# Attention: each part of the row maxima is sent as soon as it exists, not both parts after the second

## The reference

```python
x = x + xattn(layernorm(x), ctx, ctx, Wq, Wk, Wv, bv, Wo, bo)
x = x + ffn(layernorm(x), fast_b, w_fc, w_proj, u, v, gate)

# xattn: 16 heads of width 32
scores = einsum('bhsd,bhtd->bhst', qh, kh) / sqrt(32)
scores = where(mask, -inf, scores)      # mask: t >= s, but (0, 0) is kept
out = softmax(scores) @ vh              # then out @ Wo.T + bo
```

## Time and profile before

| | |
|---|---|
| time, median of 3 runs (lowest to highest) | 2607.24 us (2607.03 to 2607.67) |
| the profiled execution: its own time | 2606.1 us |
| the profiled execution: span from the first to the last instruction | 2604.4 us |
| PE busy | 2527.7 us, 97% of the span |
| DVE, ACT, POOL busy | 1764.9, 1018.5, 786.9 us |
| mean granted TensorE clock | 0.995 of full |
| one pass of the loop over the batches | 94.0 us |

### The profile page before, as it was taken

One profiled execution on the slowest core, in us unless ns is written; L12 is line 12 of the kernel. 1 busy time (PEld: TensorE's weight loads), 2 busy tenths in 40 slices (PEclk: granted clock), 3 DMA queues, 4 the chain that ended last, 5 costly groups with the idle time before them and its releaser, 6 DMA issues. The chain is left out here.

```text
span 2604.4 us, 45444 instructions
## 1 busy us (share of the span) xinstructions
PE 2527.7 (97%) x14018; PEld 1900.7 (73%) x14018; DVE 1764.9 (68%) x3492; ACT 1018.5 (39%) x1887; POOL 786.9 (30%) x1499
## 2 busy tenths in 40 slices
PE   6999999999999999999999989999999999999998
PEld 5676676677667667667667758888888888888887
DVE  5676776776776777677677665666666666666663
ACT  3433533433433443353343344333333333333332
POOL 2634743654563473474365450000000000000000
PEclk9999999999999999999999999999999999999999
DMA  5444354354354344445435441111111111111111
GB/s 159 103 129 120 103 135 136 82 155 120 89 147 134 93 128 127 120 103 135 136 81 155 117 132 34 49 48 48 48 48 48 48 48 48 48 48 48 48 52 45
DMA packets 147810, 240.78 MB, mean 92 GB/s; under 512 B 26419, under 2 KB 34611, under 8 KB 147780
## 3 DMA queue, kind: packets, MB, share of 16 engines
q1 hardware_dynamic: 143684, 239.35, 32.4%
q10 hardware_dynamic: 4096, 1.06, 0.2%
HBM read 100.85 MB, written 37.77 MB: 53 GB/s over the span
## 5 line engine op out<-in xcount | busy, mean ns | idle before, releaser
L846 ACT ACTIVATE probs<-bank 128x512 f32<-128x512 f32 x640 | 359.7, 597 | 300.6 <-PE bank L633 295.2
L1239 PE MATMUL h_bank<-xT_hi,wT 128*128 128x512 f32 x1024 | 398.4, 389 | 0.6 <-ACT projT L1270 0.6
L1240 PE MATMUL h_bank<-xT_lo,wT 128*128 128x512 f32 x1024 | 398.3, 389 | 0.0
L1254 PE MATMUL y_bank<-projT,wT 128*128 128x512 f32 x1024 | 398.3, 389 | 0.0
L1256 PE MATMUL y_bank<-projT,wT 128*128 128x512 f32 x1024 | 398.3, 389 | 0.0
L1306 ACT ACTIVATE acc<-h_bank,scale_fc 128x512 f32<-128x512 f32 x256 | 176.4, 689 | 487.6 <-PE h_bank L1243 487.6
L633 PE MATMUL bank<-stack 98*128 98x512 f32 (+3 forms) x1024 | 264.4, 342 | 30.4 <-DMA stack<-m_stage 29.8
L532 POOL TENSOR_SCALAR_AFFINE_SELECT probs<-probs 128x256 f32<-128x256 f32 (+1 forms) x640 | 226.2, 365 | 219.8 <-ACT probs L846 211.9
L608 PE MATMUL bank<-stack 96*128 96x512 f32 (+3 forms) x1024 | 264.7, 335 | 4.8 <-DVE maxima L939 4.2
L1382 DVE CAST wT<-acc 128x512 fp32r<-128x512 f32 x256 | 108.4, 423 | 214.0 <-ACT acc L1311 214.0
L935 DVE TENSOR_REDUCE maxima<-bank 128x1 f32<-128x512 f32 x256 | 175.8, 687 | 111.7 <-PE bank L612 108.5
(11 more groups left out here) (172 smaller groups left out, 4676.4 us busy)
## 6 DMA issues: line engine op xcount, KB each, us to landing
stack<-stage SPq DMA_DIRECT2D x768, 128.0 KB, 2.3
xc_rows<-in_x_dram SPq DMA_DIRECT2D x16, 1024.0 KB, 5.3
x_res<-in_x_dram SPq DMA_DIRECT2D x16, 1024.0 KB, 5.6
x<-x_res SPq DMA_DIRECT2D x64, 256.0 KB, 2.3
xc_rows<-x SPq DMA_DIRECT2D x16, 1024.0 KB, 5.7
x_res<-x SPq DMA_DIRECT2D x16, 1024.0 KB, 7.6
out_dram<-y_sb SPq DMA_DIRECT2D x64, 256.0 KB, 2.0
xc_rows<-in_ctx_dram SPq DMA_DIRECT2D x15, 1024.0 KB, 5.3
```

Source lines behind the costliest of these rows:

```text
L846: act.activation(probs[:, s[2], :], t_bank[u % 2][:, :], ACT.Exp, scale=SCALE).then_inc(exp_done, 1)
L1239: pe.matmul(h_bank[b % 2][:, :], fcT[:, k, cols], xT_hi[:, k, :], start=k == 0, stop=False)
L1240: pe.matmul(h_bank[b % 2][:, :], fcT[:, k, cols], xT_lo[:, k, :], start=False, stop=False)
L1254: pe.matmul(y_bank[j][:, :], a_hi[:, b % RING, P * j:P * j + P], projT[:, b, :], start=b == 0, stop=False)
```

## The change

ScalarE's step SEND waits for DVE's subtraction before it issues the first of two transfers. The change gives each transfer a wait of its own: the one of the rounded maxima (part 0) waits for `m_hi`, which ACT's own copy L807 raises, and the one of the rest (part 1) waits for `m_free`, which DVE's subtraction L899 raises. Nothing is added or removed but one wait and one increment of ACT's counter in each of the 64 sends. Sizes, queues, the order of the steps and what T waits for stay as they are.

```diff
                     elif s[0] == "SEND":
-                        wait_alone(act, act_passed, (m_free, i * GROUPS + s[1] + 1))
-                        for part in range(2):
+                        for part, (written, value) in enumerate(((m_hi, i * GROUPS + s[1] + 1),
+                                                                 (m_free, i * GROUPS + s[1] + 1))):
+                            wait_alone(act, act_passed, (written, value))
                             act.dma_start(stack[s[1] % 2][96 + part:97 + part, 0, :, :].bitcast(F32)
                                           .rearrange("p h (r s) -> p (h r) s", s=P),
                                           m_stage[:, part, :].bitcast(F32)).then_inc(m_stacked[s[1] % 2], 16)
```

## The result

| | before | after |
|---|---|---|
| time, median (lowest to highest, runs) | 2607.45 us (2607.03 to 2609.59, 4) | 2586.47 us (2585.95 to 2591.20, 4) |
| ratio, with its 95% interval | | 0.9922 (0.9905 to 0.9939) |
| the profiled execution: its own time, span | 2606.1, 2604.4 us | 2586.84, 2585.1 us |

What follows compares the result with a forecast made beforehand. PE was taken to bound the kernel, busy 2527.7 of 2604.4 us. Fourteen steady passes at 0.79 (11.1 us), 1.1 for the first pass and 0.2 for the last made 12.4 us: 2594.8 us, range 2588.5 to 2602.5.

Steps and rivals of the forecast that it cites:

- The steady pass: Loop passes two to fifteen: each gains 0.79 us from three groups' sends, 11.1 us over the 14.
- Group 3: Its send in each steady pass: T's first product comes sooner, winning 0.58 us of PE's 0.65 us wait.
- The low end of 0.31: Group 3's smallest gain in us per steady pass, if its second issue were as long as group 2's, 0.84.
- Group 2: Its send in each steady pass: T gains 0.54 us, but XT 3 then waits for DVE, leaving 0.11.
- Rival (a): More gained: group 2 keeps its whole 0.54 us (2588.8 us), or the first pass keeps full clock; chance 0.13.
- Group 1: Layer norm after its send in each steady pass: the pair ends 0.4 to 0.5 us sooner, PE gains 0.10.
- My cap on PE's side: At PE's product after group 1's layer norm: at most 0.19 us, 0.08 idle plus 0.11 exposed weight load.
- Group 0: Its send in each steady pass: gives nothing, since its T product does not wait for the transfer.
- The first pass: Loop's first pass gains 1.1 us: 0.2 in group 1, 0.3 in group 2, 0.58 in group 3.
- The last pass: Loop's last pass: nothing in group 3, whose maxima land with feed-forward weights; 0.2 us for the other groups.
- (b): At the sends: landing follows traffic, or the second issue grows by what was saved; no change, 2607.2 us, chance 0.13.
- (c): Slower: second transfer lands late, losing beyond 2.44 us in group 3; 2609.4 or 2629 us, chance 0.06.

Runs made afterwards that it cites:

- r1_after_again: The changed kernel unaltered, timed and profiled again: 2589.79 us over 5 runs, ratio 0.9933 to the kernel before.
- r3_after: The changed kernel unaltered, a third profile: 2590.42 us in one run.
- experiment 2: Both kernels timed again with nothing edited: the changed one 2589.79 us, the one before 2607.53 us.
- e1_pad: Against the kernel before, each transfer has its own wait but both still wait for DVE's m_free: 2607.44 us, ratio 1.0001.

## Why the forecast was right in its sign and wrong in its size

**The steady pass: the mechanism right, its terms too small.** 0.79 was forecast and 0.91 measured; for the 14 passes 11.1, and 12.1 to 13.4 over three profiles of each kernel. The sum comes that near in part by luck: the three groups give 1.01, and a loss that wasn't forecast takes 0.1 of it.

- *Group 3, 0.58:* measured 0.63 alone. The second issue took 0.51 and not 0.61 once it no longer stood directly behind the first, the upper of the two values that the forecast weighed, and the transfer landed 1.77 us behind it. The wait of 0.65 went whole. The low end of 0.31 had been made from a second issue of 0.84 and never came up.
- *Group 2, 0.11:* measured 0.15 alone, inside its 0 to 0.17. The wait for DVE took the place of most of it, as the steps said, with 0.57 us in front of the transposes. T's own wait went to nothing, where 0.3 of it was to stay, because the landing fell too, from 2.75 to 2.02 us behind its issue; XT 3 needs DVE all the same, so this was worth nothing. Rival (a)'s first half, that DVE would come sooner and give the whole, did not occur.
- *Group 1, 0.10:* measured 0.23, over its bound of 0.19. DVE's chain ended 0.8 us sooner, where 0.4 to 0.5 had been forecast, because its first two steps fell out of the time of POOL's L556 (1.36 us to 0.55). I had read them as held by L561, which starts where they end. The rule of SBUF — State Buffer, in the section on who interferes with whom, of the Trainium skill, by which a DVE instruction with two SBUF inputs is blocked until a GpSimd instruction that reads SBUF is through, holds in this trace, with L191 on the losing side: 0.65, beside L556; L190, a TENSOR_SCALAR, is held there too, with 0.67. My cap on PE's side was too tight: it counted the weight load and the idle 0.08 and nothing behind them. What the last 0.04 is I can't say.
- *Group 0, nothing:* measured a loss of 0.09 (17.36 to 17.45). I had put it at nothing since T doesn't wait there, and didn't look at what ACT's earlier issues meet: SP's, which `stack` depends on.
- *The first issue beside SP's:* in group 2 ACT loses nothing: both issues together take 1.29 us, the second 0.51 in place of 0.84. The time goes over to SP, whose 48 issues of `stack` in a pass take 29.36 us and took 28.94; in group 2 PE doesn't wait for them, in group 0 it does in the end. By the rule of Perfetto Trace Analysis, in its section on the hardware-issued DMA instruction, of the Trainium skill, in which the issuing sequencers share one descriptor generator and wait for it within the issue, the first could have grown and taken up to 1.5 us of the sum. The trace agrees that issues side by side lengthen one another, but it is SP's that grew, and the loss came in group 0: 0.09 us in each of 14 passes is 1.3.

**The first pass: the step that failed.** I put its gain at 1.1 us, with group 1's term at 0.2 because its transfer "takes 4.1 us to land, behind large loads". It was 6.7 in the profiled pair, and 3.5 to 7 over three profiles of each kernel (100.4 to 101.2 before, 94.2 to 96.9 after). The cause that I gave is wrong: no 1 MB load was in flight, but a single 16 KB packet of code. With it both bounds were wrong. A transfer that is through before the packet comes doesn't gain 0.5 but 2 us, and a half-speed stretch, worth some 1.4 to 1.7 us, goes with the idle time: 2.9 for the two here. I had the row of the clock and priced it in rival (a) as a single stretch, with a chance of 0.13 shared with another cause; rival (a)'s second half is what came. Part of the 6.7 is luck as well: where the packets fall differs from one execution to the next, and in the changed kernel's first profile both sends escaped them. What I could have done: ask for the DMA view of the 2 us in which the transfer was under way, which shows the packet, instead of naming the loads from the landing time.

**The last pass** gave 0.5 with the feed-forward block behind it, which is within the scatter of that stretch, and 0.2 had been forecast. The wait of 3.6 in group 3 fell to 1.7 in the first profile only; it is 3.7 in r1_after_again and 3.2 in r3_after. In all of them the transfer lands 5.4 to 5.8 us behind its issue, as before (5.5). What the forecast said of it, that it lands with the weights and gains nothing, stands. In the first profile a half-speed stretch at 1511.4 us, ahead of that wait, brings PE there later.

**The sum.** 0.91 in place of 0.79 is worth 1.0 us in the profiled pair (up to 2.3 with the other profiles), the first pass 5.6, the rest 0.3. On top of the 12.4 that makes 19.3 for the profiled pair, which is the difference of the spans. How far the time fell below the range is luck in part: the same kernel timed again took 2589.79 us (experiment 2), inside the range of 2588.5 to 2602.5, with a gain of 17.0, and 2590.42 in the one run of r3_after. Rivals (b) and (c) fell: the landing follows the issue, with 1.8 us in group 3 of a steady pass, under the 2.44 from which (c) would lose.

## What to carry to other kernels

Where an engine issues two transfers and both wait for the later producer, give each its own wait: the gain is one issue, about 0.5 us, wherever the critical engine waits for the pair, and it has to be followed to the next thing that is late (here 0.15 was left of 0.54 in group 2). Look also at what another engine issues where the first transfer goes now: here that cost 0.09 us of each pass, in a group that had nothing to gain. Look at the first run of a loop body by itself, since code packets there can double the landing of a small transfer, and a change of the program's length moves them into or out of its way, as a shift of the send by half a microsecond may; a first pass that differs by 6 us between two kernels is no proof for either.

## What the runs showed of the hardware

- A single 16 KB packet of kind "instruction" that starts 1.2 to 1.75 us behind the issue of an 8 KB transfer made it land at 3.4 to 4.2 us in place of 2.0 to 2.7, in 14 of 15 sends.
- In the 17 first passes PE stood idle for 1.5 us or more at one place eleven times (1.53 to 2.31 us), and ten times the granted clock fell to 0.50 there or within 2 us behind, for 3.4 us (once for 6.8). Of six idle pieces of 1.0 to 1.35 us one was followed by such a stretch. PE's busy time in the first pass is 91.9 to 92.7 us without a stretch, 93.7 to 94.3 with 3.4 us of it and 95.3 to 95.7 with 6.8: some 1.6 for each 3.4. In the 14 steady passes of each, where no idle piece was longer than 0.92 us, there was none. In the set-up it goes otherwise: idle pieces of 2.56, 1.82 and 1.50 us at 15.3, 22.7 and 27.5 us in the kernel before had no stretch behind them until 36.7.
- In the steady passes an issue of 8 KB from ACT lasts 0.51 us by itself, 0.61 directly behind another (group 3), and 0.84 when SP issues beside it as well (group 2). With a wait of its own, but both waits over at once (`e1_pad`), it is 0.53 and 0.75; in the changed kernel, where it comes 0.26 us behind the first, 0.51 in both places, and SP's issues take the longer (28.94 us in a pass before, 29.36 after).
